# Emptying the fill's last unit, and splitting the output, at other places of the step in a 32-batch masked attention kernel

## What is computed

```python
# layer 0
x = layernorm(x + (adj @ x) @ w0 + b0)
# layer 1: 8 heads of 64, adj as the mask
q, k, v = split(x @ w_qkv)
attn = softmax(where(adj == 0, -inf, q @ k.T * 64 ** -0.5))
o = (attn @ v) @ w_proj + b_proj
x = layernorm(x + o + layernorm(o) * gamma + beta)
```

## Time and profile before

| | us |
|---|---|
| median of the runs | 3750.41 |
| the profiled execution | 3750.82 |
| its span, first to last instruction | 3749.0 |

### The profile page before, as it was taken

The page is one execution under the profiler, slowest core; times in us unless marked ns, Lnnn a source line. Parts: engine busy times, 40 slices in busy tenths (PEclk is TensorE's granted clock), DMA queues, the critical chain, the costliest instruction groups (busy, mean ns, idle before and its releaser), DMA issues.

```text
span 3749.0 us, 64437 instructions
## 1 busy us (share of the span) xinstructions
PE 3614.4 (96%) x18960; PEld 2873.4 (77%) x18960; DVE 2873.4 (77%) x6681; ACT 2146.7 (57%) x4505; POOL 1529.8 (41%) x2311
## 2 busy tenths in 40 slices
PE   8999999989999999999999999999999999999996
PEld 6888888867777777777777777777777777777775
DVE  7666666647888888888888878888888788878887
ACT  4444444436666666666666666666666666666664
POOL 4555555522333333333333333333333333333334
PEclk9999999999999999999999999999999999999998
DMA  6555555531111111111111111111111111111111
GB/s 196 178 176 178 179 179 179 179 108 31 45 45 45 45 45 45 45 45 45 50 45 45 48 47 45 45 45 48 47 45 45 50 45 45 45 45 45 45 55 33
DMA packets 344957, 276.18 MB, mean 74 GB/s; under 512 B 13664, under 2 KB 275808, under 8 KB 344928
## 3 DMA queue, kind: packets, MB, share of 16 engines
q1 hardware_dynamic: 344928, 275.83, 24.6%
HBM read 141.56 MB, written 134.22 MB: 74 GB/s over the span
## 4 chain that ended last, share of the span: by engine, by line
PE 52%; DVE 20%; issue 4%; ACT 2%; DVEq 0%; POOL 0%; POOLq 0%
PE bank L773 14%; PE bank L789 10%; PE bank L737 8%; PE bank L726 7%; PE bank L807 6%; DVE probs L931 6%; DVE pt_lo L945 5%; PE bank L756 4%; PE bank L757 3%; DVE o_stats L971 2%; ACT pt_hi L851 1%; DVE ot_lo L967 1%; DVE t L999 1%; DVE k_lo L951 1%; DVE o L988 1%
## 5 line engine op out<-in xcount | busy, mean ns | idle before, releaser
L843 ACT ACTIVATE probs<-probs,bias_row 128x512 f32<-128x512 f32 x1024 | 730.3, 714 | 571.5 <-DVE bias_row L931 571.5
L945 DVE TENSOR_TENSOR pt_lo<-bank,pt_hi 128x512 fp32r<-128x512 f32 x1024 | 670.0, 686 | 175.9 <-ACT pt_hi L851 166.1
L851 ACT ACTIVATE pt_hi<-bank 128x512 fp32r<-128x512 f32 x1024 | 556.3, 595 | 224.4 <-PE bank L737 218.3
L670 POOL TENSOR_SCALAR probs<-probs,inv_sums 128x480 f32<-128x480 f32 (+1 forms) x1024 | 684.0, 681 | 0.0
L931 DVE CUSTOM_DVE_ANT_0 probs<-bank,mask_bias 128x512 f32<-128x512 f32 x1024 | 661.3, 683 | 0.0
L737 PE MATMUL bank<-ident,probs 128*128 128x128 f32 x4096 | 534.5, 273 | 17.4 <-DVE pt_lo L945 8.7
L737 PEld LDWEIGHTS bank<-ident,probs 128*128 128x128 f32 x4096 | 478.8, 141 | 90.7 <-POOL probs L670 18.5
L667 POOL TENSOR_TENSOR probs<-probs,inv_sums 128x32 f32<-128x32 f32 x512 | 122.5, 239 | 1037.8 <-DVE inv_sums L937 1037.6
L676 POOL TENSOR_TENSOR o_rstd<-o_var_eps,half_neg 128x1 f32<-128x1 f32 x256 | 156.5, 611 | 814.4 <-DVE o_var_eps L976 814.4
L756 PE MATMUL bank<-pt_hi,v 128*128 128x512 f32 x1024 | 422.8, 413 | 54.9 <-DVE k_lo L951 47.4
L773 PE MATMUL bank<-x_hi,w_hi 128*128 128x512 f32 x1024 | 411.2, 402 | 30.1 <-DVE ot L963 19.0
(11 more groups left out here) (90 smaller groups left out, 7654.2 us busy)
## 6 DMA issues: line engine op xcount, KB each, us to landing
x_in<-in_x_dram SPq DMA_DIRECT2D x32, 1024.0 KB, 5.7
ut_hi<-ut_hi_sb SPq DMA_DIRECT2D x128, 256.0 KB, 3.7
ut_lo<-ut_lo_sb SPq DMA_DIRECT2D x128, 256.0 KB, 3.6
u_beta_rows<-ub SPq DMA_DIRECT2D x32, 1024.0 KB, 4.4
x_hi<-ut_hi SPq DMA_DIRECT2D x128, 256.0 KB, 4.3
x_lo<-ut_lo SPq DMA_DIRECT2D x128, 256.0 KB, 4.6
out_dram<-o SPq DMA_DIRECT2D x128, 256.0 KB, 3.1
ub_row<-u_beta_rows SPq DMA_DIRECT2D x124, 256.0 KB, 2.9
```

What stands on the lines that cost most here:

```text
L670: pool.tensor_scalar(probs[:, k % 2, a, cols], probs[:, k % 2, a, cols], inv_sums[:, k % 4, a:a + 1], 0.0, ALU.mult, ALU.add)\
L843: act.activation(probs[:, k % 2, a, :], probs[:, k % 2, a, :], ACT.Exp, bias=bias_row[:, k % 4, a:a + 1], scale=-1.0, accum_out=sums[:, k ...
L851: act.activation(pt_hi[:, a, :, n * P:(n + 1) * P], t_bank[a][:].rearrange("p (m n) -> p m n", m=T), ACT.Copy)\
L945: dve.tensor_tensor(pt_lo[:, a, :, cols], t_bank[a][:].rearrange("p (m n) -> p m n", m=T), f32(pt_hi[:, a, :, cols]), ALU.subtract).then_i ...
```

## The change

Three edits, none of which adds or removes an instruction:

- In groups 2 and 3, ScalarE and VectorE empty unit 3 at the head of the pair's last step (k = 11 and 15), ahead of `pt_hi` and `pt_lo`, as they do in step 3 before and after. ScalarE did it behind `pt_hi`, VectorE as the last thing of the step.
- The output of a pair is split in part 1 in place of part 2: `ot_hi` and `ot_lo` go to steps 1, 9 and 13. Pair 0's stays in step 7.
- VectorE's `inverse` of step k+1 goes from the head of each step to behind `ot_sum`, the units and `add_bproj`, right ahead of `pt_lo`.

```diff
--- before.py
+++ after.py
@@ -621,9 +621,9 @@
 
 
 
-                if j == 2 and k == 6:
+                if j == 1 and k == 5:
                     return None
-                if k % T == j or (j == 2 and k == 7):
+                if k % T == j or (j == 1 and k == 7):
                     return (b - 1, PAIRS - 1) if k < T else (b, k // T - 1)
                 return None
 
@@ -892,17 +892,15 @@
 
                     def batch(b, last_part=True, more=True):
                         for k in range(STEPS):
-                            if k == 3:
+                            if k % T == 3:
                                 unit_hi(b, k, 3, more)
                             if output_at(b, k, 0) and (last_part or k >= T):
                                 ot_halves(*output_at(b, k, 0))
                             pt_hi_part(b, k)
-                            if k % T == 3 and k > 3:
-                                unit_hi(b, k, 3, more)
                             if last_part and row_at(k - 2, LN_STEP) is not None:
                                 result(b, row_at(k - 2, LN_STEP))
-                            if output_at(b, k, 2) and (last_part or k >= T):
-                                ot_hi_part(*output_at(b, k, 2))
+                            if output_at(b, k, 1) and (last_part or k >= T):
+                                ot_hi_part(*output_at(b, k, 1))
                             if k + 2 < STEPS or more:
                                 exponent(b, k + 2)
                             if k % T < 3:
@@ -1018,23 +1016,23 @@
                     def batch(b, last_part=True, more=True):
                         for k in range(STEPS):
                             ahead = k + 2 < STEPS or more
-                            if k + 1 < STEPS or more:
-                                inverse(b, k + 1)
                             if output_at(b, k, 0) and (last_part or k >= T):
                                 ot_sum(*output_at(b, k, 0))
                             if k % T in (1, 2):
                                 unit_lo(b, k, k % T - 1, more)
-                            elif k == 3:
+                            elif k % T == 3:
                                 unit_lo(b, k, 3, more)
                             if last_part and k == O_STEP[3]:
                                 add_bproj(b, 3)
+                            if k + 1 < STEPS or more:
+                                inverse(b, k + 1)
                             pt_lo_part(b, k, ahead)
                             if last_part and row_at(k - 2, LN_STEP) is not None:
                                 row_shift(b, row_at(k - 2, LN_STEP))
                             if ahead:
                                 masked_max(b, k + 2, waited=True)
-                            if output_at(b, k, 2) and (last_part or k >= T):
-                                ot_lo_part(*output_at(b, k, 2))
+                            if output_at(b, k, 1) and (last_part or k >= T):
+                                ot_lo_part(*output_at(b, k, 1))
                             if last_part and row_at(k, O_STEP) is not None:
                                 if k != O_STEP[3]:
                                     add_bproj(b, row_at(k, O_STEP))
@@ -1043,8 +1041,8 @@
                                 last_statistics(b, row_at(k - 1, LN_STEP))
                             if last_part and row_at(k, LN_STEP) is not None:
                                 add_layernorm(b, row_at(k, LN_STEP))
-                            if k % T == 2 or (k % T == 3 and k > 3):
-                                unit_lo(b, k, k % T, more)
+                            if k % T == 2:
+                                unit_lo(b, k, 2, more)
 
                     for i in range(2 * PAIRS):
                         qk_lo_part(0, i)
```

## The result

The changed kernel takes 3719.27 us, the median of 4 runs (3716.77 to 3721.55), against 3749.49 for the kernel before beside it: a ratio of 0.992 (95% interval 0.9904 to 0.9936). The prediction was 3720, with 3705 to 3738 as its range. The profiled execution has a span of 3717.4 us in place of 3749.0.

A forecast was written before the change was run, and what follows sets the result against it. TensorE, 96% busy, gains only where it stands still, chiefly 1.58 us for `k_lo` and 0.63 for `ot` per batch. Profiled 3750.8 - 31.8 - 0.4 + 1.5 = 3720.1, said as 3720; range 3705 to 3738.

The forecast's parts named there:

- the template: Step 3, already emptying its unit at the head: `pt_lo` start to attention 0.81 us, attention to next step 3.75.
- The chain of part 2 and 3: Steps 9 to 12: earlier split and later `inverse` delay VectorE's queue; step 12 begins at 17.01 in place of 18.27.
- The new wait of the statistic: Steps 10 and 14: VectorE's statistic waits 0.60 us for `add_ub`, held up on GpSimd behind the later `inverse`.
- The 4.23 for `ot_lo`: Step 9: earliest VectorE start of the moved `ot_lo`, behind T(9), after `ot_hi` at 3.57 taking 0.63 us.
- The margin of the first `ot_sum`: Step 12: `ot_sum` ends at 17.4, TensorE asks for it at 17.8, so it holds by 0.3 us.
- The sum: Per batch -1.26 + 0.27 - 0.07 = -1.06 us; 30 full batches -31.8, first batch -0.4, last with tail +1.5.
- (c): Longer chain in both groups: 0.2 to 0.45 us more each, by the `ot_sum` margin or unseen hops; 3732 to 3744, 13%.
- (b): Steps 11 and 15: the add comes in time, `q_hi` binds at 10.98; -1.44 us per batch, 3709, 12%.
- (a): Steps 11 and 15: step 3's timing holds fully, statistics not late; -2.0 us per batch, 3691, 7%.
- (d): Statistics of steps 10 and 14 behind `add_ub`: VectorE and GpSimd become the bound, batch loses 0.94 us, 3779, 4%.
- (e): Attention's second half didn't wait for the bank but something ending with it; -0.1 to +0.3 us per batch, 3747 to 3760, 4%.
- The rule weighed: Skill's exclusive VectorE/GpSimd port lock, applied to moved `ot_lo` beside `add_ub`: would change the last batch by 0.4 us, nothing else.

The follow-up runs named there:

- the unit and the inverse: Unit 3's emptying and `inverse` moved as in the change, output split left in part 2, against the kernel before: 3697.98 us, ratio 0.9857.
- two experiments: Against the kernel before: unit and split moved, `inverse` left at the head, 3710.38 us; the changed kernel with GpSimd's `add_ub` ahead of normalising, 3708.0 us.
- the first experiment: Only unit 3's emptying moved to the head of steps 11 and 15, split and `inverse` left, against the kernel before: 3699.71 us, ratio 0.9863.
- the kernel with the moved statistics: Unit and `inverse` moved, split left, row 3's first statistics and GpSimd's power moved from step 7 to 8, against the kernel before: 3674.99 us, ratio 0.9799.
- split-and-inverse kernel: Output split and `inverse` moved as in the change, unit 3's emptying left at its old place, against the kernel before: 3787.8 us, ratio 1.0097.

## Why the prediction was right, point by point

**The bound and the template.** TensorE's gaps set the time, and `k_lo` the largest of them. `pt_lo` start to attention was measured as 0.80 (2228.06 to 2228.86), attention to T(12) as 3.78, against 0.81 and 3.75.

**The chain of part 2 and 3.** Predicted and measured offsets from T(9) = 2215.63: layernorm 4.84 and 4.83, unit 1's `k_lo` 6.36 and 6.35, inverse 6.96 and 6.95, step 10's `pt_lo` 7.04 and 7.02, statistic 10.06 and 10.04, `q_lo` 11.17 and 11.15, step 11's `pt_lo` 12.45 and 12.43, T(12) 17.01 and 17.01. The new wait of the statistic is 0.54 (0.60 predicted, since I took no account of the time in which VectorE reads its accumulator, 0.08). All that the chain said of causes was then moved by itself: without the split the chain ends 0.3 earlier, with the add ahead 0.19. The 4.23 for `ot_lo` has 0.03 in it, for the way from ScalarE to VectorE, that none of the prediction's rows gives; it began at 4.22.

**What covers what.** The margin of the first `ot_sum` in step 12 was put at 0.3: it ends at 2233.05, and TensorE would ask for it at 2232.64 + 0.79 = 2233.43. Steps 8 and 12 with their late statistics cost nothing, as `pt_lo` still finds 0.33 of idleness in step 9.

**The sum.** Per batch -1.11 in place of -1.06 (step 8 -0.06, T(9) to T(12) -1.28, T(13) to T(16) +0.24, by the means); over 30 batches -33.3 in place of -31.8. The first batch gave -0.15 (predicted -0.4): its two waits gave back 0.26 each, and 0.33 was lost in steps 4 to 7, which have no fill there and for which the prediction had no term. The late inverse is not enough to explain it: with the unit and the inverse alone step 4 lasts 0.35 longer as well, but steps 4 to 7 together only 0.04. In that kernel the mean granted clock over these steps is 0.91, as before, and in the changed kernel 0.82; how much of the loss is the clock's is not shown. The last batch with the tail cost 0.6 in place of 1.5, inside its bounds. Layer 0, which the change doesn't touch, took 1.2 longer in this execution; among all the profiled kernels it differs by 1.9. -33.3 - 0.15 + 0.6 + 1.2 = -31.6, the difference of the spans. So the nearness of 3719 to 3720 is luck in part: against the prediction the full batches came out 1.5 us lower and the last 0.9, the first batch 0.25 higher and layer 0 1.2.

**The rivals.** In (c) the upper end is mis-added: 0.45 per group is 27 us, 3747 and not 3744. (b), with `q_hi` at 10.98 as the next thing late, is what two experiments made true: 3710 and 3708, where it had 3709. (a) was out of reach in the changed kernel, whose VectorE has no slack; even the unit alone stays 0.14 to 0.17 per group above it. (d) had the right place and the wrong price: nothing else was queued in front of the add. (e) fell with the first experiment.

**The rule weighed.** In the full batches the moved `ot_lo` takes 0.69 in the changed kernel and the add 1.30, so nothing meets there, as placed. In the last batch of the kernel before, the two run side by side and both are longer, the add 1.69 and `ot_lo` 1.01:

```profile
3710.98 1.01 DVE L967 TENSOR_TENSOR ot_lo<-ot,ot_hi 128x512 fp32r<-128x512 f32 x1
```

The unit alone, the unit and the inverse, and the kernel with the moved statistics split in part 2 like the kernel before, and each has one such add in the last batch, of 1.69 or 1.70. The changed kernel and the three others with the early split have none, and their adds are all under 1.35. So the meeting went with the split, the one effect that the prediction gave to the rule. What these 0.4 us were worth to the end of the last batch is not shown.

## What to carry to other kernels

Move each part of a reordering by itself on paper: here one part of three held the whole gain (about -51 us), one next to nothing (-2 us), and one cost 11 to 21 us. Before moving an operation to an earlier step, follow what is queued behind it up to the next engine's own queue: the `inverse` was harmless and so was the residual add, but the one stood in front of the other. When a wait remains after the large one is gone, look for work in front of the late operation that nobody needs yet, and for a place where the same engine waits.

## What the runs showed of the hardware

A longer wait of TensorE can cost more than its length. Each of the 30 full batches of the split-and-inverse kernel has a silence of 2.25 to 2.29 us in step 11, and in 12 of them the granted clock fell to 1.2 GHz right behind it, at 1.6 us each; with 1.96 to 1.99 us in the kernel before, in none. Why it fell in these 12 and not in the others stays open.

A small operation is not always small. VectorE's inverse costs 0.07 between `k_lo` and `pt_lo` (2227.99 to 2228.06), but behind the second `ot_sum` it moves `pt_lo` from 0.72 to 0.92 behind that sum (2190.37 to 2191.29 in the kernel with the moved statistics). In the kernel before, at the head of step 12:

```profile
2249.40 0.69 DVE L963 TENSOR_TENSOR ot<-bank,ot 64x512 f32<-64x512 f32 x1 [2.17 <-ACT ot L873]
2250.12 1.29 DVE L945 TENSOR_TENSOR pt_lo<-bank,pt_hi 128x512 fp32r<-128x512 f32 x2
```

The Trainium skill, VectorE: DVE Perf Modes, section "Two Vector instructions with no wait between them", has a model for it, in which a quadrant is a group of 32 partitions: an instruction whose start quadrant differs from that of the last one on the same memory starts only when all earlier ones are finished. `ot_sum` of the second head starts in partition 64, the inverse and `pt_lo` in partition 0, and the inverse touches no PSUM, so by that model both are held, and one was before. The trace agrees: the inverse starts 0.04 behind the end of `ot_sum` (2190.37 + 0.69, then 2191.10) and `pt_lo` 0.02 behind the end of the inverse (2191.10 + 0.17, then 2191.29), while in step 11 `pt_lo` starts 0.08 before the end of the inverse (2227.99 + 0.15, and 2228.06). It was no loss in the full batches, where the steps 0, 4, 8 and 12 have fill: step 12 lasts 5.54 in the unit alone and 5.54 in the unit and the inverse.
